# A decoder layer on one core: when the cross weights are loaded, and when a group's second row is normalised, at the end of self-attention

## What is computed

```python
x = _layernorm(x + _L0_attn_ref(x, ...))              # causal, 16 heads, latent size 72
x = _layernorm(x + _L0_xattn_ref(x, ctx, ctx, ...))   # context of 120 tokens, 16 heads of 64
x = _layernorm(x + _L0_ffn_ref(x, ...))               # 16 experts, 32 tokens each per sequence, and a shared one

def _L0_attn_ref(x, latent_w, latent_b, Wd_w, Wd_b, out_w, out_b):
    Wdkv = x @ latent_w + latent_b
    q = jnp.einsum('btc,hcl->bhtl', x, Wd_w) + Wd_b[None, :, None, :]
    scores = jnp.einsum('bhtl,bsl->bhts', q, Wdkv) / jnp.sqrt(d_head)
    attn = jax.nn.softmax(jnp.where(causal, scores, -jnp.inf), axis=-1)
    z = jnp.einsum('bhts,bsl->bhtl', attn, Wdkv)  # heads side by side
    return z @ out_w + out_b
```

## Time and profile before

| | us |
|---|---|
| median of 3 runs | 3178.88 |
| lowest, highest | 3176.5, 3179.21 |
| the profiled execution's own time | 3177.35 |
| its span in the profile | 3175.5 |

### The profile page before, as it was taken

How to read it: one execution, slowest core, us unless ns; L and a number is a source line. 1 busy time by engine, 2 the same in 40 slices (tenths; PEclk the granted TensorE clock), 3 DMA queues, 4 the chain that set the end, 5 groups by cost and what they waited for, 6 DMA issues and landing times. The chain is left out here.

```text
span 3175.5 us, 78664 instructions
## 1 busy us (share of the span) xinstructions
PE 3087.6 (97%) x22624; PEld 2900.1 (91%) x22624; DVE 2257.3 (71%) x6562; ACT 2142.5 (67%) x6926; POOL 1590.1 (50%) x2912
## 2 busy tenths in 40 slices
PE   6999999999999998999999999999979999999998
PEld 5999999999999987999999999999868888889998
DVE  6777777777777877778877788788755455544665
ACT  6888888888887877787877877778734444442222
POOL 4666766666666765333333333333546666653000
PEclk8999999999999999999999999999989999999999
DMA  6444444444444440111111211111235444533333
GB/s 181 117 123 124 125 124 121 120 121 125 123 111 116 129 134 24 54 57 45 63 45 48 64 45 48 61 44 54 101 103 120 99 97 100 129 56 85 121 124 106
DMA packets 193684, 300.70 MB, mean 95 GB/s; under 512 B 33856, under 2 KB 134080, under 8 KB 192704
## 3 DMA queue, kind: packets, MB, share of 16 engines
q1 hardware_dynamic: 168768, 262.91, 27.8%
q0 software_dynamic: 24576, 33.57, 6.2%
HBM read 116.02 MB, written 67.11 MB: 58 GB/s over the span
## 5 line engine op out<-in xcount | busy, mean ns | idle before, releaser
L962 POOL TENSOR_SCALAR ca_prob<-ca_prob,ca_inverse 128x120 f32<-128x120 f32 x1024 | 354.7, 365 | 631.7 <-DVE ca_inverse L1264 629.7
L665 ACT ACTIVATE sa_prob<-sa_prob,sa_shift 128x128 f32<-128x128 f32 (+1 forms) x1024 | 453.5, 460 | 2.6 <-DVE sa_shift L718 2.6
L1210 ACT ACTIVATE ca_prob<-bank,ca_shift 128x120 f32<-128x120 f32 x1024 | 353.7, 366 | 5.7 <-DVE ca_shift L1258 3.5
L460 POOL TENSOR_SCALAR sa_prob<-sa_prob,sa_inverse 128x128 f32<-128x128 f32 x512 | 198.5, 388 | 231.6 <-DVE sa_inverse L726 217.8
L718 DVE CUSTOM_DVE_ANT_0 sa_prob<-bank,sa_mask 128x128 f32<-128x128 f32 (+1 forms) x1024 | 304.7, 352 | 7.0 <-PE bank L138 2.7
L136 PE MATMUL bank<-sa_ow,sa_y_hi 128*128 128x256 f32 x1024 | 279.6, 304 | 0.0
L136 PE MATMUL bank<-sa_kvT_a,sa_q 128*128 128x128 f32 (+1 forms) x1024 | 251.6, 281 | 16.5 <-DMA sa_q<-sa_q_tile 16.4
L138 PE MATMUL bank<-sa_kvT_b,sa_q 112*128 112x128 f32 (+1 forms) x1024 | 261.9, 281 | 0.0
L749 DVE TENSOR_TENSOR sa_pT_lo<-bank,sa_pT_hi 128x384 fp32r<-128x384 f32 x512 | 258.0, 543 | 1.8 <-ACT sa_pT_hi L650 1.8
L138 PE MATMUL bank<-sa_ow,sa_y_lo 112*128 112x256 f32 x1024 | 258.9, 283 | 0.0
L462 POOL TENSOR_SCALAR sa_prob<-sa_prob,sa_inverse 128x256 f32<-128x256 f32 x512 | 245.0, 478 | 0.0
(11 more groups left out here) (258 smaller groups left out, 12030.0 us busy)
## 6 DMA issues: line engine op xcount, KB each, us to landing
sa_q<-sa_q_tile SPq DMA_DIRECT2D x128, 288.0 KB
sa_q<-sa_q_tile SPq DMA_DIRECT2D x160, 112.0 KB
mid_x2T<-ca_x2T SPq DMA_DIRECT2D x32, 512.0 KB, 2.9
ex_sx<-mid_x2T SPq DMA_DIRECT2D x32, 512.0 KB, 3.3
sa_q<-sa_q_tile SPq DMA_DIRECT2D x304, 32.0 KB, 4.5
sa_xT_raw<-in_xT SPq DMA_DIRECT2D x32, 256.0 KB, 2.8
sa_q<-sa_q_tile SPq DMA_DIRECT2D x32, 256.0 KB
sa_x_res<-in_x SPq DMA_DIRECT2D x32, 256.0 KB, 2.8
```

What stands on the lines that cost most here:

```text
L460: pool.tensor_scalar(prob[:, r, hh, 0:P], prob[:, r, hh, 0:P], inverse[:, r, 2 * hh:2 * hh + 1], 1.0, ALU.mult, ALU.mult)
L665: act.activation(prob[:, r, hh, cols], prob[:, r, hh, cols], ACT.Exp, bias=shift[:, r, n:n + 1], scale=-1.0, accum_out=total[:, r, n:n + 1 ...
L962: ins = pool.tensor_scalar(prob[:, r, t, hh], prob[:, r, t, hh], inverse[:, r, n:n + 1], 1.0, ALU.mult, ALU.mult)
L1210: act.activation(prob[:, r, t, hh], SC[g % 2][:, n * S:n * S + S], ACT.Exp, bias=shift[:, r, n:n + 1], accum_out=total[:, r, n:n + 1]).the ...
```

## The change

Two edits at the end of self-attention. First, in `load_cross` SyncE waits before each of the three weight loads for a PV product: wv for that of the drain's slot 0, wk for slot 1's, wq for slot 3's (it keeps the wait for the last q product). Second, in the drain, and there alone, the second row's pair of steps, GpSimd's normalisation and SyncE's store, stands four slots later: at slots 9 and 25 in place of 5 and 21. All instructions are the same ones, and TensorE's, VectorE's and ScalarE's order is as before.

```diff
+    def x1_at(J):
+
+        return (X1[0], X1[1] + 4) if isinstance(J, int) and J == SA_BODIES else X1
+
...
             sp.wait_ge(q_mm, QT * GROUPS)
             for n in range(len(CROSS) - 1):
+                sp.wait_ge(pv_mm, upto_slot(SA_BODIES, (0, 1, 3)[n] - PL))
                 sp.dma_start(cross.raw[n].rearrange("p (k n) -> p k n", k=KC),
...
-            for c, i in due(J, m, X1):
+            for c, i in due(J, m, x1_at(J)):
                 need(sp, x1_done, upto_row(J, c, i, TT))
...
-            for c, i in due(J, m, X1):
+            for c, i in due(J, m, x1_at(J)):
                 need(pool, x1_out[i], upto_group(J, c - 1, 16))
```

## The result

The changed kernel takes 3189.18 us, the median of 8 runs (3188.22 to 3192.01), against 3179.16 us for the kernel before, the median of 8 runs beside it (3176.28 to 3181.27). The ratio is 1.0035, interval 1.0026 to 1.0044: 8 to 14 us slower. The prediction was 3185.9 us in a range of 3179.0 to 3189.0. The direction was the one forecast, the size was not: about +10 to +11 us in place of +7.0, and the median lies 0.2 us over the range.

The account below looks back on a forecast made before the run. The prediction took TensorE, busy 97% of the span, to bound the kernel. Its terms -0.7 (A) - 2.1 (B) + 9.8 (C) = +7.0 us, from the median of 3178.88, gave 3185.9 us, range 3179 to 3189.

Parts of the forecast that it names:

- A: TensorE's 3.48 us stop in drain slot 0's PV product: later weight loads shorten it, -0.7 us (0 to -1.4).
- Rival 1: Weight loads starve TensorE of instructions, so the stop at slot 0 goes: +1.4 us in all, 3180.3 us; chance 0.2.
- B: Slot 5 to 9 move: TensorE's 2.62 us wait at the last transposes goes, -2.1 us (-4.1 to -1.5).
- VectorE's gain is the path's: 2.18 + 0.41: After the last transposes, VectorE's saved idling and shorter split reach TensorE in full, 2.6 us.
- the clearing: At slot 9, normalisation makes GpSimd's clearing of k 0.9 us late for cross-attention's first scores; 0.5 us counted.
- C: Slot 21 to 25 move: TensorE stops 7.65 us at cross slot 16, plus 2.1 low clock: +9.8 us (7.7 to 10.5).
- Rivals 2 and 3: Rival 2 (0.12): C has no effect, -2.8, 3176.1 us; rival 3 (0.08): C half covered, +3.0, 3181.9 us.

Follow-up runs that it names:

- e1_loads: Kernel before plus only the three waits on the weight loads, second rows left at slots 5 and 21: 3179.42 us, ratio 0.9999.
- e4_slot23: Kernel before with the last row's normalisation and store at slot 23 in place of 21, loads as before: 3183.66 us, ratio 1.0012.
- e7_allloads: Kernel before plus the three weight-load waits, and the first two rows' and contexts' loads also waiting for slot 0's PV product: 3178.14 us, ratio 0.9997.
- e6_exit: Kernel before with TensorE's self-attention loop ending one body earlier, rows and loads as before: 3171.76 us, ratio 0.9977.
- e10: Kernel before with 148 semaphore increments put ahead of TensorE's first matmul: 3184.74 us, ratio 1.0016.
- e11: Kernel before with 64 semaphore increments put ahead of TensorE's first matmul: 3191.08 us, ratio 1.0035.
- e12: Kernel before with TensorE's self-attention loop beginning one body later, rows at slots 9 and 21, ScalarE making the y copy from slot 7 on: 3169.10 us, ratio 0.9966.
- e2_slot9: Kernel before with only the early group's second row moved from slot 5 to 9, loads as before: 3179.41 us, ratio 0.9998.
- e3_slot25: Kernel before with only the last row moved from slot 21 to 25, loads as before: 3190.52 us, ratio 1.0034.

## Why the prediction was wrong

**A was right in kind, and in size partly by luck.** Forecast -0.7 (0 to -1.4), and a stop of 2.1 to 3.5 us at the same instruction; seen -1.3, a stop of 3.21. The argument that the weights are issued after the stop has begun held: with their waits alone the stop is 3.48. But the forecast's gain was a shorter stop, and left the low clock as it was. The stop gave 0.3 us in the change and nothing in e1_loads; the other 1.0 us came in the low clock behind it, and e4_slot23 has it without the waits. Rival 1 fell; all loads together are worth 1.1 us of the stop (e7_allloads).

The Trainium skill's rule on branches ("Runtime: NRT & Kernel Launch", section "Instruction fetch mechanics") fits: the stop moved with the exit of the loop in e6_exit. It speaks of a branch out of the code that has been fetched and not of every exit, and the prediction took this one for such a branch because the loop ends there. Three kernels left this loop with no stop (e10, e11, e12), and in these the place of the code was what had changed. The same section says that code comes in blocks of 16 KiB, and the agreement of 140,544 and 9,472 bytes is what one would see by it.

**B is the step that failed, in its sign.** Forecast -2.1, bounds -4.1 and -1.5; seen +1.8 in the change and +2.2 alone. Up to slot 8's PV product it was right: the last multiplications took 0.37 us each, the wait of 2.62 us was gone, and TensorE was 2.45 us ahead at that product (1200.45 in the trace of before), where "VectorE's gain is the path's: 2.18 + 0.41" had said 2.6. What failed is that this gain was carried on to the end of the stretch, with only the clearing against it. The projection right behind needs GpSimd's copy as well as VectorE's part of y, and the sum put the copy at nothing. It took 5.63 us in place of 1.60, and TensorE waited for it 1.45 us and ran at the low clock behind: from 2.45 ahead it came to 1.8 behind by 1208, in e2_slot9 to 0.6 behind. With the copy on ScalarE the stretch up to 1208 gives -1.74 in four kernels alike, inside the bounds. The rows had two warnings. The 0.41 us, "its next split took 2.77 where its like took 2.36", was GpSimd's copy having its turn, so that winning it back meant shutting the copy out. And the prediction itself put the 2.42 us of a GpSimd multiplication down to VectorE's split of wv, and didn't ask which GpSimd instruction would meet the next split. The 0.5 us for later clearing didn't come at all: GpSimd waited 1.72 us ahead of it, and the first scores 1.06 us for VectorE, as before.

The Trainium skill has a rule that bears on this ("SBUF — State Buffer", section "Who interferes with whom"): a VectorE instruction with two inputs in SBUF contends with a GpSimd instruction that reads SBUF, over a pair of ports that they share under an exclusive lock. The trace agrees in part: the copy of 0.61 us was stretched to 5.63. What the rule doesn't give is that the copy missed its turn between the two splits.

**C was right.** Forecast a stop of 7.65 us for a DMA and 2.1 of low clock, +9.8; seen 7.63 and 10.15 in all, so 2.5 for the clock. The chain from normalisation to landing was forecast at 5.88 us and is 6.0. That the stop was met to 0.02 us is luck, since the same chain took 6.3 us in e3_slot25 and 6.9 in e4_slot23. Rivals 2 and 3 fell with the stop of 7.63 us: beyond the slack of 5.3 us nothing was covered.

**The sum.** -0.7 - 2.1 + 9.8 = +7.0 was forecast; -1.3 + 1.8 + 0.6 + 10.15 = +11.2 is in the trace, and +10.0 between the medians. B makes 3.9 of the 4.2 us. The 0.6 between B and C is a low clock behind a wait of 2.84 us that the one trace of before happened not to have, and that eight of the thirteen later traces show; so it isn't the change's own. The forecast's own top of 3187.9 had B at -1.5; with B's bound at zero, since what limits TensorE behind the move isn't in the trace of before, it would have been 3189.4, and would have held the time, though not B, which came out beyond zero.

## What to carry to other kernels

Before counting a longer instruction or an idle stretch of one engine as a gain, look at who had his turn in it: here VectorE's split was 0.4 us longer because a GpSimd copy got in, and without that the copy took 5.6 us on the path. A chain through memory (normalise, store, load, transpose) can be added up from its rows, here to within 0.1 to 1.0 us (5.9 worked out, 6.0, 6.3 and 6.9 measured), and a move by four slots should be set against its slack first. Before a step of 1 to 2 us between two traces is put down to an edit, look whether a low clock came behind the same wait in the one and not in the other. And when an edit changes the length of an engine's code, compare the waits at the ends of later loops as well: here they were worth 6 us, though no work of that loop had been touched.

## What the runs showed of the hardware that I had not expected

- A GpSimd copy of 16x512 elements, 0.61 us undisturbed, took 5.63 us beside two VectorE splits of 2.35 us each, though there was a gap of 0.5 us between them, with a VectorE instruction of 0.68 us with one input in a bank, in two kernels alike; ScalarE made it in 0.63 us at the same place.
- A stop behind the exit of a hardware loop (2.4 to 3.8 us in the traces, 6.3 with the low clock behind it where the stop is 3.48) and waits of 0.8 to 1.4 us at each jump back of another loop went away when the engine's code was moved by 148 instructions, or by a multiple of 16 KiB and 148 instructions. The waits at the jumps back carry the name of another engine, which had ended 3.5 us before; the branch instruction itself is on record with 2.6 to 3.1 us in place of 0.35.
- A semaphore increment alone on TensorE costs 0.15 us (84 more of them put its first matmul 12.86 us later).
- ScalarE, too, stops behind its loop over cross-attention: 1.5 to 2.0 us in ten kernels, 2.8 to 3.4 in the four where its code is longer by the copy.
- The same wait of 2.30 us on TensorE had the low clock behind it in eight traces of fourteen, at a cost of 1.5 to 1.6 us, and full clock in six.
- The low clock (granted 0.50, the 1.2 GHz level) came behind a stop as short as 1.45 us, where two of 1.49 and 1.55 us stood close ahead of it, and behind one of 2.07 us. It cost 1.8 us behind 2.07 and 2.2 to 2.8 behind the stops of 3.5 us and more.
